# Partition calls for a token softmax, router logits taken through the product over heads, and token tiles without a halo

## The reference, cut to what matters

```
q, k, v = split(layernorm(x) @ w_qkv)           # [b, H, n, 64] each, q scaled by 1/8
q_l, k_l = means of q and k over 16 tokens       # 64 landmarks a head
attn1 = softmax(q @ k_l^T); attn2 = softmax(q_l @ k_l^T); attn3 = softmax(q_l @ k^T)
z = moore_penrose_inverse(attn2)                 # 6 iterations
out = attn1 @ z @ (attn3 @ v)
out = out + conv13(out)                          # 13 taps along the tokens, one filter a head
x   = x + out @ w_fc + b_fc

xn = layernorm(x)
logits = xn @ router_w.T
weights, selected = sparsemixer_eval(logits, 0.01)      # top 2 of 8
for e in range(8):
    h = silu(xn @ w_gate[e].T) * (xn @ w_up[e].T)
    x = x + weight_of(e) * (h @ w_down[e].T)
```

## Time and profile before

| | |
|---|---|
| median of 3 runs | 1094.46 us (1092.64 to 1095.97) |
| profiled execution, its own time | 1094.18 us |
| its span, first to last instruction | 1092.5 us |
| mean granted clock of TensorE | 0.994 |
| HBM traffic | 62 GB/s over the span |

### The profile page before, as it was taken

How to read it: one execution, slowest core, us unless ns; L and a number is a source line. 1 busy time by engine, 2 the same in 40 slices (tenths; PEclk the granted TensorE clock), 3 DMA queues, 4 the chain that set the end, 5 groups by cost and what they waited for, 6 DMA issues and landing times.

```text
span 1092.5 us, 21456 instructions
## 1 busy us (share of the span) xinstructions
PE 1059.0 (97%) x8358; PEld 850.3 (78%) x8358; DVE 634.9 (58%) x1369; ACT 320.3 (29%) x489; POOL 329.3 (30%) x326
## 2 busy tenths in 40 slices
PE   4999999999999999999999999999999999999996
PEld 4888888888889756666666766788787877878895
DVE  7458745555549776677778678765434334344332
ACT  4433222233326422342332332331212122121210
POOL 6000000000026323225535534553243333333332
PEclk9999999999999999999999999999999999999998
DMA  9300000000300400311421323335433333323122
GB/s 337 135 1 1 1 1 1 1 1 1 99 3 1 161 36 30 108 68 60 146 74 54 108 78 117 106 115 112 89 48 51 43 47 51 50 46 46 21 29 24
DMA packets 48252, 68.27 MB, mean 62 GB/s; under 512 B 8224, under 2 KB 41504, under 8 KB 47136
## 3 DMA queue, kind: packets, MB, share of 16 engines
q1 hardware_dynamic: 34288, 46.83, 13.8%
q0 software_dynamic: 13440, 16.93, 9.0%
q10 hardware_dynamic: 432, 3.24, 0.7%
HBM read 41.43 MB, written 26.59 MB: 62 GB/s over the span
## 4 chain that ended last, share of the span: by engine, by line
PE 89%; DVE 5%; POOL 2%; issue 2%; ACT 0%; POOLq 0%; DVEq 0%; ACTq 0%
PE ps L1886 19%; PE ps L1487 10%; PE ps L1446 10%; PE ps L1929 10%; PE ps L1785 9%; PE ps L1732 8%; PE ps L1777 5%; PE ps L1870 2%; PE ps L1547 2%; PE ps L1554 2%; PE ps L1849 1%; PE ps L1420 1%; PE ps L1923 1%; PE ps L1502 1%; PE ps L1677 1%
## 5 line engine op out<-in xcount | busy, mean ns | idle before, releaser
L1886 PE MATMUL ps<-mem 128*128 128x256 f32 (+1 forms) x1152 | 221.9, 345 | 0.0
L1886 PEld LDWEIGHTS ps<-mem 128*128 128x128 f32 x1152 | 190.1, 191 | 27.2 <-issue 7.5
L615 POOL DMA_INDIRECT out<-mem x60 | 102.2, 1703 | 185.5 <-DVE mem L1306 145.9
L1294 DVE TENSOR_TENSOR mem<-mem,ps 128x512 f32<-128x512 f32 x66 | 45.4, 688 | 146.5 <-PE ps L1886 128.8
L1732 PE MATMUL ps<-mem 128*128 128x512 f32 x288 | 129.5, 593 | 0.0
L836 ACT ACTIVATE mem<-ps 128x512 f32<-128x512 f32 x66 | 39.4, 597 | 277.1 <-PE ps L1886 240.5
L1785 PE MATMUL ps<-mem 128*128 128x256 f32 x512 | 119.5, 387 | 0.0
L1487 PE MATMUL ps<-mem 128*128 128x256 f32 x512 | 117.4, 383 | 0.0
L1446 PE MATMUL ps<-mem 128*128 128x256 f32 x512 | 116.1, 384 | 0.0
L580 POOL TENSOR_TENSOR mem<-mem,small 128x1024 f32<-128x1024 f32 x36 | 68.6, 1905 | 156.4 <-DVE small L1231 77.1
L1929 PE MATMUL ps<-mem 128*128 x480 | 113.7, 380 | 0.9 <-DVE mem L1294 0.9
(11 more groups left out here) (232 smaller groups left out, 1306.1 us busy)
## 6 DMA issues: line engine op xcount, KB each, us to landing
mem<-w_gu SPq DMA_DIRECT2D x9, 1024.0 KB, 5.8
mem<-xs_d SPq DMA_DIRECT2D x22, 260.0 KB, 2.9
mem<-x SPq DMA_DIRECT2D x8, 512.0 KB, 7.9
mem<-x SPq DMA_DIRECT2D x32, 128.0 KB, 2.3
out<-mem SPq DMA_DIRECT2D x32, 128.0 KB, 1.7
mem<-w_down SPq DMA_DIRECT2D x8, 512.0 KB
xnt_d<-mem ACTq DMA_DIRECT2D x3, 1056.0 KB, 5.6
mem<-xnt_d SPq DMA_DIRECT2D x3, 1056.0 KB, 6.2
```

Source lines behind the costliest of these rows:

```text
L615: pool.indirect_dma_start(out=out_rows, out_offset=bass.IndirectOffsetOnAxis(ap=rows_to.bitcast(U32), axis=0), in_=ys[:, r % YRING], in_of ...
L1294: dve.tensor_tensor(hid[:, n % 2], sil[:, n % 2], bank(2 + n % 2), ALU.mult).then_inc(s("m_hid"), 1)
L1886: mm = pe.matmul(bank(2 * c + n % 2)[:, i * size:(i + 1) * size], w[:, k, c, f * P:(f + 1) * P], xst[:, a % 2, k, 0:size], start=(k == 0), ...
```

## The change

Three parts.

*Token softmax.* The part over the partitions is done by GpSimd with `partition_all_reduce` on 128x256, once for the maxima (`c1_token_max`) and once for the sums (`c1_token_sum`), and the result stands in every partition. The six transposes a period and VectorE's two column reductions are gone. The inverse sums are now 256 reciprocals a partition (`rin`), and since they lie along the columns, `utb` is scaled by them: `c1_tokens_out` is on VectorE, and ScalarE copies `v3`.

*Router.* The logits are linear in the rows before normalisation up to the mean and the deviation. The router's columns are centred (`router_columns`), the share of `x` in the logits, `lx`, is computed once at the front from the transposed normalised input (L1469 to L1483 of the changed kernel), and the share of attention comes with the products: `w_fc` times the router (`wfr`) is set beside `w_fc` as eight more columns (`DX` = 264), goes through `value_product` and `c2_y`, and `rows_out` adds `lx`. `choices` multiplies by the inverse deviation. The transposes and matmuls for logits in the token steps are gone, and `value_product` runs in 16 rounds of two pairs.

*Tiles.* A tile has 128 new tokens, and the band makes 140 columns (`TS`) out of it, six before and six behind. There are 32 tiles. ScalarE copies the columns that the tile before has not written, and VectorE's `edges(q)` adds the twelve that overlap with it. `c2_conv` and `c2_y` wait for it (`c2_edge`), the 140 columns of eight head pairs lie in banks 4, 5 and 7, and the steps of the lists move.

```
-TO = P - 2 * HALO
-CT = -(-N // TO)
+TS = P + 2 * HALO
+CT = N // P
+DX = D + E
-CHOSEN = [i + 3 for i in DONE[:LATE]] + [QT, QT + 2, QT + 4]
+CHOSEN = [i + 1 for i in DONE]
+COUNTED = [i + 2 for i in DONE[:LATE]]
+PLACED = [i + 3 for i in DONE[:LATE]] + [QT + 3, QT + 5]
...
+            def c1_token_max(m):      # GpSimd
+                pool.wait_ge(s("c1_mx"), m + 1)
+                if m >= 2:
+                    pool.wait_ge(s("c1_sub"), m - 1)
+                pool.partition_all_reduce(pmr[:, m % 2], pmx[:, 0], P, bass.bass_isa.ReduceOp.max).then_inc(s("c1_gmax"), 1)
+            def c1_token_sum(m):
+                pool.wait_ge(s("c1_sum"), m + 1)
+                if m >= 1:
+                    pool.wait_ge(s("c1_r3"), m)
+                pool.partition_all_reduce(psr, sums[:, m % 2], P, bass.bass_isa.ReduceOp.add).then_inc(s("c1_gsum"), 1)
+            for m in range(1, NP2 - 1):
+                if m + 2 < NP2:
+                    c1_token_max(m + 2)
+                c1_token_sum(m + 1)
...
             def c1_less_max(m):       # VectorE
-                dve.wait_ge(s("c1_bc"), m + 1)
-                dve.tensor_tensor(e3, e3, bank(5)[:, 0:2 * P].unsqueeze(1).to_broadcast([P, RT, 2 * P]), ALU.subtract)
+                dve.wait_ge(s("c1_gmax"), m + 1)
+                dve.tensor_tensor(e3, e3, pmr[:, m % 2].unsqueeze(1).to_broadcast([P, RT, 2 * P]), ALU.subtract)
             def c1_inverse_sums(m):
-                ch.link(dve.tensor_reduce(s3[:, u:u + 2], bank(4)[:, 2 * P:4 * P].rearrange("p (u t) -> p u t", u=2), AX, ALU.add))
-                dve.reciprocal(r3[:, u:u + 2], s3[:, u:u + 2]).then_inc(s("c1_r3"), 1)
+                dve.wait_ge(s("c1_gsum"), m + 1)
+                if m >= 1:
+                    dve.wait_ge(s("c1_utb"), m)
+                dve.reciprocal(rin, psr).then_inc(s("c1_r3"), 1)
+            def c1_tokens_out(m):
+                dve.wait_ge(s("c1_r3"), m + 1)
+                dve.wait_ge(s("c1_ut"), m + 1)
+                dve.tensor_tensor(utb, bank(6).rearrange("p (k c) -> p k c", k=KD), rin.unsqueeze(1).to_broadcast([P, KD, 2 * P]),
+                                  ALU.mult).then_inc(s("c1_utb"), 1)
             for m in range(1, NP2):
                 if m + 1 < NP2:
                     c1_less_max(m + 1)
+                c1_inverse_sums(m - 1)
+                c1_tokens_out(m - 1)
...
+            for c in range(2):        # TensorE, ahead of the key products
+                for k in range(KD):
+                    for b in range(B):
+                        mm = pe.matmul(bank(c)[32 * b:32 * b + 32], rwc[:, k], xnts[b][:, k, 512 * c:512 * c + 512], ...)
+            for j in range(J):
+                for k in range(KD):
+                    mm = pe.matmul(bank(2)[:, j * E:(j + 1) * E], wfct[:, k, j * P:(j + 1) * P], rw[:, k * E:(k + 1) * E], ...)
+            for t in range(RT):
+                mm = pe.transpose(bank(4 + t // 4)[:, t % 4 * P:(t % 4 + 1) * P], lgx[:, t * P:(t + 1) * P], idt)
...
             def rows_out(m):          # VectorE
+                dve.tensor_tensor(logits[:, m - GROUPS[group_of(m)][0]], bank(6)[:, D:DX], lx[:, m], ALU.add)
                 dve.tensor_tensor(x1[:, u], bank(6)[:, 0:D], xr[:, m % XR], ALU.add).then_inc(s("c2_x1"), 1)
+            def edges(q):
+                dve.wait_ge(s("c2_cvt"), q + 1)
+                ...
+                        last = dve.tensor_tensor(columns, columns, product[:, :, :, low:high], ALU.add)
+                last.then_inc(s("c2_edge"), 1)
             def token_step(i):
+                if 0 <= i - 3 < QT and (i - 3) % CT:
+                    edges(i - 3)
...
             def c2_conv(q):           # TensorE
-                    pe.wait_ge(s("c2_cvt"), cvt_count(q - 1))
+                    pe.wait_ge(s("c2_cvt"), q)
+                    if q >= 2:
+                        pe.wait_ge(s("c2_edge"), edges_done(q - 1))
             def c2_y(m):
-                pe.wait_ge(s("c2_cvt"), cvt_count(y_step(m) - 3))
+                pe.wait_ge(s("c2_edge"), edges_done(m + 1 if m % CT < CT - 1 else m))
-                    mm = pe.matmul(bank(6)[:, 0:D], cvt[:, j, at_:at_ + P], pm[:, b, j], ...)
+                    mm = pe.matmul(bank(6)[:, 0:DX], cvt[:, j, at_:at_ + P], pm[:, b, j], ...)
```

More of the change, by code:

```diff
@@ L59 @@
 NG = len(GROUPS)
-PAIRS = [sum(n // 2 for _, n in GROUPS[:g]) for g in range(NG + 1)]
-LOGITS = [min(g, NG - 3) + 2 * (g > NG - 3) + max(0, g - (NG - 2)) for g in range(NG + 1)]
 XR, X1 = 4, 8
@@ L155, in y_before @@
     return sum(y_step(m) < i for m in range(MT))
-def cvt_count(q):
-    return q + 1 + sum(CT * b + RINGT // TO <= q for b in range(B))
 def sent_before(g, u, v):
@@ L437, in _ @@
             batch_columns(1)
-            for i in range(QT + 4):
+            for i in range(QT + 5):
                 m = y_tile(i - 1)
@@ L917, in normalise, with router_columns @@
                                           ALU.subtract, ALU.mult).then_inc(s("a_xn_dve"), 1)
+            def router_columns():
+                dve.wait_ge(s("r_mm"), 1)
+                rwk = rw[:, :].rearrange("p (k e) -> p k e", k=KD)
+                ch.link(dve.scalar_tensor_tensor(out=rwk, in0=bank(7)[:, 0:E].unsqueeze(1).to_broadcast([P, KD, E]), scalar=-1.0 / D, in1=rwk,
+                                                 op0=ALU.mult, op1=ALU.add))
+                ch.step(dve.tensor_copy(rwx, rwk.unsqueeze(2).to_broadcast([P, KD, 4, E])))
+                dve.tensor_tensor(brw, rwk, bcol.unsqueeze(2).to_broadcast([P, KD, E]), ALU.mult).then_inc(s("r_made"), 1)
             row_statistics(0)
@@ L1395, in _, with sums_down @@
             halves = (slice(0, M), slice(M, P))
+            def sums_down(to, columns):
+                for k in range(KD):
+                    mm = pe.matmul(bank(7)[:, to:to + E], ones[:, :], columns[:, k], start=(k == 0), stop=(k == KD - 1))
+                return mm
+            pe.wait_ge(s("consts"), 1)
+            pe.wait_ge(s("r_in"), 32)
+            sums_down(0, rw[:, :].rearrange("p (k e) -> p k e", k=KD)).then_inc(s("r_mm"), 1)
             for b in range(B):
@@ L1931, in down @@
                 mm.then_inc(s("m_down"), 1)
-            for i in range(QT + 2):
+            for i in range(QT + 3):
                 token_step(i)
-            last = QT + 2
-            c2_tp(NG - 2, 0)
-            pe.wait_ge(s("c2_cvt"), cvt_count(QT - 1))
-            c2_late_lg(NG - 2, 0)
+            last = QT + 3
             x_columns(0)
@@ L1941, in _ @@
             c2_y(MT - 1)
+            c2_counts(NG - 2)
             pe.wait_ge(s("e_w_in"), 16)
```

485 lines of the change are left out of this document (208 added, 277 removed).

## The result

Four runs of the changed kernel gave 1083.84 us in the median (1083.38 to 1085.28), beside 1094.31 before. The ratio is 0.9914, interval 0.9902 to 0.9926. Two more measurements on other chips gave 0.9935 (0.9918 to 0.9952) and 0.9904 (0.9889 to 0.9919). Forecast were 1074 us and a range of 1062 to 1090. The sign and the range held, the size did not: 10.5 us instead of 20.6.

What follows compares the result with a forecast made beforehand. The prediction took TensorE's work (busy 1059.0 of 1092.5 us) as the bound. Token softmax -8.2, router +8.8, products +2.0 and stage 2 -23.2 gave -20.6 us: forecast 1074 us, range 1062 to 1090.

Steps and rivals of the forecast that it cites:

- Token softmax, what goes: Token softmax: three pairs of transposes removed, 0.75 us a period, 12.0 us over 16 periods.
- What comes: Token softmax: 32 GpSimd calls over the partitions on 128x256, taken at 3 us each, hidden up to 5.2 us.
- The loop: Token softmax: sum call, maximum call, subtraction and reciprocal in sequence, two calls plus 4.1 us against a 14.54 us period.
- estimate of 31 us a call: Token softmax, long-call rival (chance 0.12): an eighth of the skill page's reduction time per call, ending at 1795 us.
- The wait at the start: Start of token softmax: TensorE waits once for the first tokens, 3.8 us.
- Router block: Front of the kernel: added router matmuls and transposes, with 0.4 us for waits, cost +8.8 us.
- "+2.0": Product stage: VectorE's two evictions set the pace, +1.0 us, and a late eviction wait adds +1.0.
- The choice between the ends for 140 columns: Token steps: a 140-column convolution taken at 2.03 us, +2.3 in all; the other end was 1.74, -7.0.
- The logits: Token steps: transposes, matmul blocks and waits for logits removed, -16.9 us.
- The 2 us for holds in group steps: Token steps: VectorE held by GpSimd, 2 us added over 7 groups.
- The tail: End of token steps: waits of 3 us for the last convolution and 2 for bank 6, no difference from before.
- The rival "VectorE becomes late": VectorE delays TensorE: +8 us in the token softmax, 1 us in each of 7 groups; 1089 us, chance 0.14.

Runs made afterwards that it cites:

- fourfold run: The changed kernel with each of the 32 partition calls issued four times; 1142.30 us in one execution.
- run of the part alone: The kernel before with only the first part of the change (partition calls, scaled tokens on VectorE, v3 on ScalarE); 1090.42 us, ratio 0.9969.
- rows-first run: The changed kernel with tile 30's edge sums, output tiles 28 and 30 and group 6's counts ahead of choices and inverse deviations on VectorE; 1077.92 us, ratio 0.9868.
- edges-first run: The changed kernel with the inverse sums and tile 30's edge sums ahead of group 6's choices on VectorE; 1080.31 us, ratio 0.9886.

## Why the prediction was right in kind and wrong in size

**The bound.** Right: TensorE's busy time fell by 18.6 us, and no stage is bound otherwise, except for the starts and ends between stages, which is where the forecast failed. The rows of the table add up to -10.6 us, 10.0 short of the forecast: 8.5 in token steps and tail, 3.9 in the token softmax, 1.0 at the router, 0.6 at the two ends, less 4.0 gained in inverse and products.

**Token softmax, what goes.** "0.75 us" a period was 0.66. I took the distance over each pair of transposes, but the wide block beside one is shorter for it: the similarities of the earlier trace rows take 6.91 us up to the transposes (171.26 to 178.17), and 7.00 with none behind them (181.70 to 188.70). 14 periods: 9.2 us, not 10.5. The end of the stage gave 0.5, not 1.5; another 1.0, three pairs of transposes for the last sums, lies in the next row of the table.

**What comes.** The call was estimated at 3 us; it is 1.43 and 1.79. The loop was right, as the fourfold run shows. The Trainium skill's figure (GPSIMD Engine Reference, 3.2 Cross-partition) is for another instruction, and the estimate of 31 us a call made from it is far off for this one: the measurement decides. The wait at the start was 3.17 us (3.8 forecast). The clock behind it was not in the sum: 1.7 us in this execution, 2.9 in the run of the part alone, none in two others of the changed kernel. This is the second step that failed: the start was priced as a wait at the full clock. Together -4.3 instead of -8.2, with the 0.42 us wait for the first exponentials.

**Router block.** 3.57 + 3.60 + 1.83 = 9.0 us, and 0.8 in the key products behind it. Without the clock it is 8.16 (forecast 8.8). Right, but for the clock.

**Products.** "+2.0" was nothing: from the first value product to the first token similarity 19.39 us, 19.42 before. A round with two evictions takes 2.11 us, where I expected VectorE to set a slower pace; the late eviction wait did not come. The 2.0 us less in this row of the table stand ahead of the products, in the inverse (70.17 us, 72.14 before); 1.0 of them are the transposes named above. The other 1.0 I haven't followed, and no term of the forecast had it: it is luck.

**Token steps.** Similarities 3.53, convolutions 2.05 (2.03 forecast), output products 3.67 (3.66): right. The choice between the ends for 140 columns was right; weight loading does not set the pace. The logits were overpriced by the overlap with the neighbours, as above: an output product beside transposes is 3.45 us where it is 3.55 in the earlier trace rows, and the similarity behind it 3.44, not 3.53, in the trace of before:

```profile
444.87 3.62 PE L1785 MATMUL ps<-mem 128*128 128x256 f32 x16
448.32 3.60 PE L1732 MATMUL ps<-mem 128*128 128x512 f32 x8
451.76 0.60 PE L1745 MATMUL ps<-ids,mem 128*128 128x128 f32 x4
```

That is 0.1 us in each of 16 groups, 1.6 us. The 2 us for holds in group steps did not come: TensorE has no wait for edges in a step with a similarity.

**The tail.** This is the step that failed: "3 us for the last convolution and 2 for bank 6, against the old tail's 2.0 us ... no difference". The two waits were 5.0 and 3.8 us, with 1.7 and 2.7 us of lower clock behind them, 13.1 us; all idle time and lower clock of the tail together went from 5 to 14.3 us, where the forecast had no difference. I had named what stands in the queue (group steps and their choices) and then set 3 and 2 us for the tail without adding up that queue; the queue ahead of the edge sums was choices and inverse sums, 7 us from 672.6, of which some 2.5 us came from holds (1.55 us for an instruction of 0.19, while GpSimd weighed and added biases). The rows-first run gives 7.3 of the 9.4 us back by order alone, 3.4 as waits and 3.9 as busy time that the lower clock had added, so the order is shown as the cause of most of it. The edges-first run alone gives 4.4 back, all as clock, of which 1.7 follow from its shorter wait. That the remaining 2.2 us against before are VectorE's routing work with nothing beside it is argued only.

That the time fell inside the range is partly luck: the range was wide enough for a rival whose places were others. The rival "VectorE becomes late" had the mechanism, at another place: I put it at 1 us in each of seven group steps and 8 us in the softmax; it came once at the start and twice at the end.

## What to carry to other kernels

Where an edit makes TensorE depend on a further queue, price the wait in the last step apart, by what stands in that queue then: in the middle a similarity covered it, and at the end nothing did. Put the small instruction that the bounding engine waits for ahead of the long chain that it doesn't, and check what the third engine has queued in the meantime. Add to a wait that the clock may be low behind it: here it was in four of seven traces behind 3.17 us, in eight of ten behind 3.8 us and in nine of nine behind 5.0 us, for 1.5 us and more each time. And to price narrow instructions between wide ones, compare whole periods, not the distance over the narrow ones.

## What the runs showed of the hardware that was not expected

- A partition call on 128x256 takes 1.43 us (maximum) and 1.79 us (sum), and 3.03 us beside VectorE's subtraction of 2048 elements, which itself kept its 2.28. There the wait was GpSimd's. It is not so for every pass: in each period one VectorE pass of 512 elements beside the maximum call takes 0.98 us in place of 0.69 (177.82 us in the changed kernel's trace).
- Beside other GpSimd work, small VectorE instructions of two SBUF inputs are held while GpSimd passes over 1024 elements and 256. VectorE in the rows-first run, GpSimd at work from 674.30 to 678.24:

```profile
673.19 0.16 DVE L1174 SCALAR_TENSOR_TENSOR small<-small 128x4 f32<-128x4 f32 x1
...
673.78 2.51 DVE L1174 SCALAR_TENSOR_TENSOR small<-small 128x4 f32<-128x4 f32 x1
676.32 0.64 DVE L1175 SCALAR_TENSOR_TENSOR small<-small 128x4 f32<-128x4 f32 x1
```

- Matmuls with 32-column weights run four at a time when the four quarters follow each other (3.57 us for sixteen of 512 columns), and one at a time (0.97 us each) with a full matmul between them.
- After the same wait of 3.17 us with the same code around it the granted clock fell in one of three traces of the changed kernel (8.70 or 7.01 us for the next block). At the router block it fell in all three, for 1.6 to 3.3 us of loss, without any wait: what ran there were the 8-column matmuls and transposes. Behind the 1-column matmuls at 150 us it fell without a wait in 15 of 16 traces. So a few us of this kernel's time differ from execution to execution. The Trainium skill (TensorE: Matmul & The Clock Gate, Part 1) says that the place where the clock rises, early in sustained matmul work, varies from run to run; here it is the fall, in the middle of a kernel, and it varies too.
